# The two expert layers of a top-2 MoE: from split weights in SBUF to weights fetched for each tile

## The chip, the cores and the metric

The kernel runs on one core of one Trainium2 chip. Its time is device microseconds (us) of one execution; the number that counts is the median of several executions, 302.83 us before the change (302.64 to 302.89 in 3 runs). Engines: PE is TensorE (PEld its weight loads), DVE VectorE, ACT ScalarE, POOL GpSimd, SP SyncE; a q behind the name is the engine's sequencer.

## The reference, cut to what matters

Eight batches of 512 tokens with 128 features pass through a small recurrence, which is residual and normalised; then each token goes to its two best experts of eight.

```
x = x + LN(recurrence(LN(x)))                  # two 128x128 layers, relu, a scan
logits = LN(x) @ gate                          # 8 experts, the best 2, softmax of the two
for each token, for each of its 2 experts e:   # w0, w1: 8 x 128 x 512, wo: 8 x 512 x 128, float32
    y = (silu(h @ w0[e]) * (h @ w1[e])) @ wo[e]
x = x + LN(sum of weight * y over the 2)
```

Everything is float32, and the first recurrence and gate decide which experts are taken, so products have to be close to float32.

## The kernel before, in words

Batches are worked off one after another in the **attention part**: layer norm, transpose, two matmuls with a scan between them, residual, second norm, logits, choice of two experts, and for each token its place in a table of rows sorted by expert. POOL sends the rows of each batch there by indirect DMA (`send_row`, L457, 8 per batch). When enough rows of an expert are there, 128 of them make a **tile**: 71 tiles in all (`TILES`). DVE writes for each tile its first row and its expert's first weight chunk (`tile_row_i`, `tile_chunk_i`, semaphore `s_table`, once per phase), and SP loads the rows of a tile into one of 16 ring buffers (`load_tile`, L330 to L333).

The first three batches run before the **loop over slots**: each engine's block first lists that part by hand, in a fixed order, then runs `for k, s, t in slots()`, where slot t works on tile t and its neighbours and, through `a_slot`, on a piece of batches k+3 and k+4 (eight slots per k). Every engine works strictly in its written order, so one waiting instruction holds all behind it.

In a slot PE does: transpose the rows of tile t (`turn_tile`, L1626); both first layers of tile t-1 (`two_layers`); a piece of the attention part; the transposes of `gated` of tile t-2 (`turn_gated`, L1668); the last layer of tile t-3 (`last_layer`, L1684). The product of float32 numbers in the first layers is made from three matmuls of float32r numbers (`layer`, L1631 to L1633): high rows by high weights, low rows by high weights, high rows by low weights. So all weights of w0 and w1 are split before the loop: ACT rounds them (`round_w`, L589), POOL (w0) and DVE (w1, `split_rest`) subtract (L273), and PE with ACT (`low_part`, L1699 and L1701, `take_low`, L595) makes three of the eighths of w1's low part. The rows stand in the array (stationary) and 512 weight columns stream past, so the result has tokens on partitions and must be transposed before the last layer, which contracts over the 512 features. ACT copies x as high part (`first_part`), DVE makes the low part (`rest_part`, L1267); ACT applies silu (`gate_curve`, L633), DVE multiplies (`times_gate_curve`, L1274), ACT copies the transposed result (`gated_turned`, L638) and weighs the output (`take_y`, L648). POOL sends the weighted rows to their pair (`send_y`, L470). After the last tile the pairs are loaded, summed, normalised and added to x.

`fill` (L1693) issues matmuls whose results nobody uses. `late_power` (L435, L438) is the reciprocal root of a variance on POOL; the residual of batch 3, the first in the loop, waits for one.

## Time and profile before

| | us |
|---|---|
| median of 3 runs | 302.83 |
| the profiled execution | 302.5 |
| its span, first to last instruction | 300.8 |
| PE / DVE / ACT / POOL busy in it | 258.3 / 203.0 / 186.8 / 172.5 |
| first transpose of a tile on PE starts at | 58.7 |
| last `take_y` on ACT starts at | 286.4 |

Times inside the profile count from the span's start. Matmuls are pipelined, and their durations overlap: what one costs is the distance from its start to the next start. A float32 matmul appears as two instructions (L1684, x568 for 71 tiles of four matmuls); a float32r matmul and a transpose appear as one. PEclk is the granted clock of TensorE in tenths of full speed (2.4 GHz).

### The profile page before, as it was taken

The page shows a single profiled execution, that of the slowest core. Times are in us where ns is not written, and L with a number is a line of the kernel's source. Part 1 is how long each engine was busy: PE and PEld are TensorE (multiplying, and loading weights), DVE is VectorE, ACT ScalarE, POOL GpSimd, SP SyncE. Part 2 cuts the span into 40 slices and gives each one's busy share as a digit, 9 for nine tenths or more (in the row PEclk, how much of TensorE's full clock was granted, in tenths as well). Part 3 has the DMA queues.
Part 4 walks back from the last instruction along what each step waited for, and adds up shares of the span by engine and source line. Part 5 has one row for each costly group of instructions (what it writes and reads, how often), then busy time and mean ns, then how long its engine had stood idle before and what let it go on. Part 6 is the DMA issues. An engine that isn't in the chain of part 4 may idle for free.

```text
span 300.8 us, 6844 instructions
## 1 busy us (share of the span) xinstructions
PE 258.3 (86%) x1633; PEld 214.1 (71%) x1633; DVE 203.0 (67%) x944; ACT 186.8 (62%) x451; POOL 172.5 (57%) x195
## 2 busy tenths in 40 slices
PE   0646596879999999999999999999999999999800
PEld 0225263448878698898988889888988988888700
DVE  3787998678597559458755955785653433888745
ACT  3666397327665765767684566666566566568681
POOL 7019577757238775874776577777532333357540
PEclk9995559589999999999999999999999999999985
DMA  5999711302111122112212211343333115602137
GB/s 146 153 384 321 210 50 52 89 29 68 50 47 45 46 74 72 44 56 71 74 44 72 74 46 49 97 108 91 100 81 86 43 31 199 263 17 91 49 99 209
DMA packets 28132, 29.57 MB, mean 98 GB/s; under 512 B 4570, under 2 KB 21180, under 8 KB 28096
## 3 DMA queue, kind: packets, MB, share of 16 engines
q1 hardware_dynamic: 22832, 20.04, 23.4%
q0 software_dynamic: 4544, 8.97, 9.3%
q8 instruction: 16, 0.26, 0.4%
q10 hardware_dynamic: 720, 0.13, 0.3%
q14 instruction: 20, 0.16, 0.2%
HBM read 17.53 MB, written 12.05 MB: 98 GB/s over the span
## 4 chain that ended last, share of the span: by engine, by line
PE 71%; DVE 13%; ACT 6%; POOL 4%; issue 4%; DMA 1%; POOLq 0%; DVEq 0%; ACTq 0%
PE bank L1684 19%; PE bank L1631 10%; PE bank L1632 10%; PE bank L1633 10%; PE bank L1668 10%; PE bank L1626 3%; PE bank L1582 2%; PE bank L1554 2%; ACT sb_row L576 1%; PE bank L1575 1%; POOL expert_rows L457 1%; DMA sb_x<-in_L_attn_x 1%; DVE sb_early L864 1%; PE bank L1566 1%; ACT sb_early L548 1%
## 5 line engine op out<-in xcount | busy, mean ns | idle before, releaser
L470 POOL DMA_INDIRECT pair_rows<-sb_y_rows,sb_y_pair x71 | 70.4, 991 | 60.2 <-ACT sb_y_rows L648 41.6
L457 POOL DMA_INDIRECT expert_rows<-sb_row,sb_place x64 | 64.0, 1001 | 23.8 <-issue 16.6
L1684 PE MATMUL bank<-sb_w_raw,sb_gatedT 128*128 x568 | 75.0, 275 | 0.0
L1684 PEld LDWEIGHTS bank<-sb_w_raw,sb_gatedT 128*128 128x128 f32 x568 | 69.1, 192 | 0.2
L1274 DVE TENSOR_TENSOR sb_w_raw<-bank,sb_w_raw 128x512 f32<-128x512 f32 x71 | 48.9, 689 | 29.9 <-PE bank L1633 21.6
L638 ACT ACTIVATE sb_gatedT<-bank 128x512 f32<-128x512 f32 x71 | 42.3, 596 | 37.0 <-PE bank L1668 36.9
L1631 PE MATMUL bank<-sb_w_parts,sb_x_hi 128*128 x142 | 63.0, 444 | 0.3 <-DVE sb_w_raw L1274 0.2
L1632 PE MATMUL bank<-sb_w_parts,sb_x_lo 128*128 x142 | 56.4, 397 | 0.0
L1633 PE MATMUL bank<-sb_w_parts,sb_x_hi 128*128 x142 | 56.1, 395 | 0.0
L633 ACT ACTIVATE sb_w_raw<-bank 128x512 f32<-128x512 f32 x71 | 42.5, 599 | 7.2 <-PE bank L1633 6.0
L1267 DVE TENSOR_TENSOR sb_x_lo<-bank,sb_x_hi 128x128 fp32r<-128x128 f32 x71 | 20.2, 285 | 35.0 <-ACT sb_x_hi L628 34.7
L1668 PE MATMUL bank<-sb_ident,sb_w_raw 128*128 128x128 f32 x284 | 42.9, 273 | 1.1 <-ACT sb_gatedT L638 0.8
L1668 PEld LDWEIGHTS bank<-sb_ident,sb_w_raw 128*128 128x128 f32 x284 | 34.3, 140 | 10.6 <-issue 3.2
L628 ACT ACTIVATE sb_x_hi<-bank 128x128 fp32r<-128x128 f32 x71 | 19.6, 276 | 34.3 <-PE bank L1626 34.2
L1633 PEld LDWEIGHTS bank<-sb_w_parts,sb_x_hi 128*128 128x128 f32 x142 | 26.9, 189 | 6.6
L1631 PEld LDWEIGHTS bank<-sb_w_parts,sb_x_hi 128*128 128x128 f32 x142 | 27.3, 192 | 6.0 <-issue 3.0
L1632 PEld LDWEIGHTS bank<-sb_w_parts,sb_x_lo 128*128 128x128 f32 x142 | 27.2, 192 | 2.9
L648 ACT ACTIVATE sb_y_rows<-bank,sb_y_weight 128x128 f32<-128x128 f32 x71 | 25.7, 363 | 1.5 <-PE bank L1684 1.0
L1626 PE MATMUL bank<-sb_ident,sb_taken_rows 128*128 128x128 f32 x71 | 19.9, 281 | 0.7 <-ACT sb_w_parts L595 0.7
L273 POOL TENSOR_TENSOR sb_w_parts<-sb_w_raw,sb_w_parts 128x512 fp32r<-128x512 f32 x8 | 10.8, 1383 | 14.4 <-ACT sb_w_parts L589 14.4
L576 ACT ACTIVATE sb_row<-sb_x,sb_nm,sb_rs 128x128 f32<-128x128 f32 x32 | 14.3, 488 | 7.0 <-DVE sb_nm L820 7.0
L1566 PE MATMUL bank<-sb_w_outT,sb_early 128*128 128x128 f32 x64 | 11.6, 339 | 6.8 <-DVE sb_early L864 6.8
(194 smaller groups left out, 358.8 us busy)
## 6 DMA issues: line engine op xcount, KB each, us to landing
sb_taken_rows<-expert_rows SPq DMA_DIRECT2D x71, 65.5 KB, 1.9
sb_w_raw<-in_L_ffn_w SPq DMA_DIRECT2D x2, 2048.0 KB, 15.1
sb_w_raw<-pair_rows SPq DMA_DIRECT2D x3, 1024.0 KB, 7.5
out_dram<-sb_x SPq DMA_DIRECT2D x3, 512.0 KB, 3.8
pair_rows<-sb_y_rows,sb_y_pair POOLq DMA_INDIRECT x71, 2.3
sb_x<-in_L_attn_x SPq DMA_DIRECT2D x4, 256.0 KB, 5.9
expert_rows<-sb_row,sb_place POOLq DMA_INDIRECT x64, 2.4
expert_rows<-sb_pad_row SPq DMA_DIRECT2D x8, 65.5 KB
```

The source lines that it names most:

```text
L457: pool.indirect_dma_start(expert_rows[:, :], bass.IndirectOffsetOnAxis(ap=place[b % ROWS][:, k, j:j + 1], axis=0), row[b % ROWS][:, j, :], ...
L470: pool.indirect_dma_start(pair_rows[:, :], bass.IndirectOffsetOnAxis(ap=y_pair[group % 2][:, t % PAIRS:t % PAIRS + 1], axis=0), y_rows[slo ...
L633: act.activation(silu[t % 2][:], p_l1[:], ACT.Silu).then_inc(c["silu"], 1)
L638: act.activation(gatedT[t % 2][:], p_gatedT[:], ACT.Copy).then_inc(c["gatedT"], 1)
L648: act.activation(y_rows[t % Y_SLOTS][:], p_y[t % 2][:, 0:D], ACT.Copy, scale=y_weight[group % 2][:, t % PAIRS:t % PAIRS + 1]).then_inc(c[" ...
L1274: dve.tensor_tensor(gated[t % 2][:], p_l2[:], silu[t % 2][:], ALU.mult).then_inc(c["gated"], 1)
L1626: pe.transpose(p_xeT[:, 0:P], taken_rows[:, t % RING, 0:D], ident[:]).then_inc(c["xeT_ps"], 1)
L1631: pe.matmul(to, x_hi, w_hi, start=True, stop=False)
L1632: pe.matmul(to, x_lo, w_hi, start=False, stop=False)
L1633: return pe.matmul(to, x_hi, w_lo, start=False, stop=True)
L1668: last = pe.transpose(p_gatedT[:, n * P:(n + 1) * P], gated[t % 2][:, n * P:(n + 1) * P], ident[:])
L1684: last = pe.matmul(p_y[t % 2][:, 0:D], gatedT[t % 2][:, n * P:(n + 1) * P], wo.rearrange("p o d -> p (o d)"), start=(n == 0), stop=(n == F ...
```

## The change

Splitting is gone: `w_parts`, `round_w`, `take_low`, `low_part`, `split_rest` and the subtractions on POOL are removed. In `layer` the weights now stand in the array and the rows stream past, with plain float32 matmuls, four per layer of 128 weight columns each; the result comes out with features on partitions, so `turn_gated` and `gated_turned` are removed, and `last_layer` takes `gated` itself, one slot earlier. The weights of a tile are brought together (w0 and w1 of its expert, 128 partitions by 2 times 2 KB) from `w_raw` in SBUF to one of four buffers `w_now` by a DMA that ACT issues two tiles ahead (`chunk_of`, `fetch_w`). `silu`, `gated` and the pairs that are loaded at the end get memory of their own instead of that of `w_raw`. Three `fill`s change, batch 3's second statistics move ahead of the loop, and POOL's power for it too. The diff, without the removed helpers:

```diff
+W_RING = 4
-        silu = [w_raw[:, n * F:(n + 1) * F] for n in (0, 1)]
-        gated = [w_raw[:, n * F:(n + 1) * F] for n in (2, 3)]
+        xeT = pair("xeT", [P, P])
+        silu, gated = pair("silu", [P, F]), pair("gated", [P, F])
+        w_now = [sb(f"w_now{n}", [P, 2, F]) for n in range(W_RING)]
+        pairs_early = sb("pairs_early", [P, 6 * pair_cols])
...
 @block.gpsimd   # before: the four subtractions stood ahead of the sends
-            for n in range(W_SPLITS // 2):
-                pool.wait_ge(s_w_hi, n + 1)
-                first, size = w_split(n)
-                subtract_hi(pool, first, size // 2)
-                subtract_hi(pool, first + size // 2, size // 2).then_inc(s_w0_lo, 1)
             for b in (0, 1):
                 for n in range(K * G):
                     send_row(b, n)
+            late_power(2, 0, ROOT2, mv2[ROOT2 % 2], sd2[ROOT2 % 2], rs2[ROOT2 % 2])
...
 @block.scalar   # eight round_w and three take_low removed from the part before the loop
             def first_part(t):
                 if is_tile(t):
                     act.wait_ge(c["xeT_ps"], t + 1)
-                    act.activation(x_hi[t % 2][:], p_xeT[:, 0:P], ACT.Copy).then_inc(c["x_hi"], 1)
+                    act.activation(xeT[t % 2][:], p_xeT[:, 0:P], ACT.Copy).then_inc(c["xeT"], 1)
+            def chunk_of(t):
+                if not is_tile(t):
+                    return
+                if t == 0:
+                    act.wait_ge(s_w_in[0], 16)
+                    act.wait_ge(s_w_in[1], 16)
+                for p in range(PHASES + 1):
+                    if t == first_tile(p):
+                        act.wait_ge(s_table, p + 1)
+                chunks[t] = act.value_load(tile_chunk_i[0:1, t:t + 1], min_val=0,
+                                           max_val=(E - 1) * FC)
+
+            def fetch_w(t):
+                if not is_tile(t):
+                    return
+                wait(act, c["l2_ps"], t - W_RING + 1)
+                both = w_raw[:, 0:2 * WCOLS].rearrange("p (w c f) -> p w c f", w=2, f=D)
+                act.dma_start(w_now[t % W_RING][:].rearrange("p w (c f) -> p w c f", f=D),
+                              both[:, :, bass.ds(chunks[t], FC), :]
+                              ).then_inc(s_w_now[t % W_RING], 16)
...
             relu(3)
+            chunk_of(0)
+            fetch_w(0)
+            chunk_of(1)
+            fetch_w(1)
             act.activation(unused[:], eps[:], ACT.Silu)
             normalise1(4, 0, G)
-            take_low(2)
 
             for k, s, t in slots():
                 first_part(t)
                 take_y(t - 4)
                 tanh_of_gaps(t)
                 a_slot(k, s, 0)
+                chunk_of(t + 2)
                 gate_curve(t - 1)
+                fetch_w(t + 2)
                 a_slot(k, s, 1)
-                gated_turned(t - 2)
                 a_slot(k, s, 2)
...
 @block.vector
             scan(3)
-            split_rest(LOW_BY_PE, 4)
             top(2)
             choose(2)
-            split_rest(4, 6)
+            start2(3)
             put(2)
             offset1(5)
 
             for k, s, t in slots():
-                rest_part(t)
-                if t == 0:
-                    split_rest(6, 8)
-                elif t == 2:
+                if t == 2:
                     table_start(1)
...
 @block.tensor
-            def layer(to, x_hi, x_lo, first_chunk):
-                w_hi, w_lo = (w_parts[:, bass.ds(first_chunk, FC), part, :] for part in (0, 1))
-                pe.matmul(to, x_hi, w_hi, start=True, stop=False)
-                pe.matmul(to, x_lo, w_hi, start=False, stop=False)
-                return pe.matmul(to, x_hi, w_lo, start=False, stop=True)
+            def layer(to, x, w):
+                for n in range(FC):
+                    last = pe.matmul(to[:, n * P:(n + 1) * P], w[:, n * P:(n + 1) * P], x,
+                                     start=True, stop=True)
+                return last
...
-                n = t % 2
+                n, w = t % 2, w_now[t % W_RING]
+                pe.wait_ge(s_w_now[t % W_RING], 16 * (t // W_RING + 1))
                 wait(pe, c["silu"], t)
-                layer(p_l1[:], x_hi[n][:], x_lo[n][:], chunks[t]).then_inc(c["l1_ps"], 1)
+                layer(p_l1, xeT[n][:], w[:, 0, :]).then_inc(c["l1_ps"], 1)
                 wait(pe, c["gated"], t)
-                if t == 0:
-                    pe.wait_ge(s_w1_lo, 1 + LOW_BY_PE)
-                layer(p_l2[:], x_hi[n][:], x_lo[n][:],
-                      chunks[t] + W_CHUNKS).then_inc(c["l2_ps"], 1)
+                layer(p_l2, xeT[n][:], w[:, 1, :]).then_inc(c["l2_ps"], 1)
...
             times_gate(1)
-            low_part(0)
+            fill(p_l1, 6)
             ranks(1)
             turn1(3)
-            low_part(1)
+            fill(p_l1, 4)
             times_w_in(3)
...
             ranks(2)
-            low_part(2)
-            pe.wait_ge(s_w1_lo, LOW_BY_PE)
             for k, s, t in slots():
                 if is_tile(t - 1):
-                    pe.wait_ge(c["x_lo"], t)
+                    pe.wait_ge(c["xeT"], t)
                 turn_tile(t)
                 if t == 0:
                     pe.wait_ge(a["x1"], 3)
-                    fill(p_y[0], 3)
+                    fill(p_y[0], 2)
                 two_layers(t - 1)
                 a_slot(k, s, 0)
                 chunk_of(t)
-                if t == TILES:
-                    last_layer(t - 3)
-                    turn_gated(t - 2)
-                else:
-                    turn_gated(t - 2)
-                    last_layer(t - 3)
-                if t == 1:
-                    pe.wait_ge(a["x1"], 3)
-                    fill(p_gatedT, 3)
+                last_layer(t - 2)
                 a_slot(k, s, 1)
```

## Rows read from the trace of the kernel before

**Rows 1.** The page: busy us per engine, then the granted clock in 40 slices.
```profile
PE 258.3 (86%) x1633; PEld 214.1 (71%) x1633; DVE 203.0 (67%) x944; ACT 186.8 (62%) x451; POOL 172.5 (57%) x195
PEclk9995559589999999999999999999999999999985
```

**Rows 2.** Stretches: length, PE busy (instructions), granted clock, DMA share, GB/s.
```profile
140.00:160.00 20.00, 20.00 (x136) 1.00 0.18 55
253.00:256.00 3.00, 3.00 (x23) 1.00 1.02 415
```

**Rows 3.** PE in order of time, one tile: start us, us, engine, line, instruction.
```profile
166.77 1.06 PE L1684 MATMUL bank<-sb_w_raw,sb_gatedT 128*128 x8
167.66 0.27 PE L1626 MATMUL bank<-sb_ident,sb_taken_rows 128*128 128x128 f32 x1
...
169.18 0.60 PE L1668 MATMUL bank<-sb_ident,sb_w_raw 128*128 128x128 f32 x4
169.61 0.61 PE L1684 MATMUL bank<-sb_w_raw,sb_gatedT 128*128 x4
```

**Rows 4.** The chain that ended last, one piece: start us, us, what.
```profile
86.20 0.11 PE bank L1626
```

**Rows 5.** DVE in order of time, before the loop and its first slot.
```profile
23.66 0.98 DVE L820 SCALAR_TENSOR_TENSOR sb_nm<-sb_mv,sb_rs 128x4 f32<-128x4 f32 x1
31.33 0.98 DVE L918 TENSOR_TENSOR sb_row<-sb_top 128x4 f32<-128x4 f32 x1
...
42.97 0.15 DVE L918 TENSOR_TENSOR sb_row<-sb_top 128x4 f32<-128x4 f32 x1
...
52.53 0.66 DVE L273 TENSOR_TENSOR sb_w_parts<-sb_w_raw,sb_w_parts 128x512 fp32r<-128x512 f32 x1
...
63.75 1.13 DVE L879 SCALAR_TENSOR_TENSOR sb_x<-bank,sb_rs,sb_x 128x128 f32<-128x128 f32 x4 [1.27 <-POOL sb_rs L438]
```

**Rows 6.** POOL in order of time, before the loop and its first slots.
```profile
27.35 4.94 POOL L273 TENSOR_TENSOR sb_w_parts<-sb_w_raw,sb_w_parts 128x512 fp32r<-128x512 f32 x4 [0.27 <-ACT sb_w_parts L589]
35.48 1.35 POOL L457 DMA_INDIRECT expert_rows<-sb_row,sb_place  x1 [3.19 <-DVE sb_place L971]
...
55.61 1.09 POOL L457 DMA_INDIRECT expert_rows<-sb_row,sb_place  x1 [0.30 <-issue]
...
62.66 1.05 POOL L438 TENSOR_TENSOR sb_rs<-sb_sd,sb_minus_half 128x4 f32<-128x4 f32 x1
```

**Rows 7.** PE in order of time, around the start of the loop.
```profile
58.67 0.47 PE L1626 MATMUL bank<-sb_ident,sb_taken_rows 128*128 128x128 f32 x1 [0.69 <-ACT sb_w_parts L595]
...
60.29 0.77 PE L1631 MATMUL bank<-sb_w_parts,sb_x_hi 128*128 x1
...
70.87 1.02 PE L1554 MATMUL bank<-sb_early,sb_w_inT 128*128 128x512 f32 x2
```

**Rows 8.** ACT in order of time, before the loop.
```profile
50.12 0.59 ACT L595 ACTIVATE sb_w_parts<-bank 128x512 fp32r<-128x512 f32 x1
50.60 0.69 ACT L563 ACTIVATE sb_early<-bank,sb_b_in 128x512 f32<-128x512 f32 x1
```

**Rows 9.** SP's row loads: instruction, count: ns min/median/max, first and last start us.
```profile
L331 SPq TENSOR_LOAD <-sb_tile_row_i x71: 263/268/577, 52.5 to 239.4; - x71
L333 SPq DMA_DIRECT2D sb_taken_rows<-expert_rows x71: 332/333/1237, 53.6 to 240.1; - x71
```

**Rows 10.** The page, DMA issues: KB each, median us from issue to landing.
```profile
sb_taken_rows<-expert_rows SPq DMA_DIRECT2D x71, 65.5 KB, 1.9
sb_early<-pair_rows SPq DMA_DIRECT2D x1, 512.0 KB, 3.4
```

**Rows 11.** All engines in order of time, the last tiles.
```profile
281.54 1.05 PE L1684 MATMUL bank<-sb_w_raw,sb_gatedT 128*128 x8
281.81 0.69 DVE L1274 TENSOR_TENSOR sb_w_raw<-bank,sb_w_raw 128x512 f32<-128x512 f32 x1 [1.14 <-PE bank L1633]
...
286.41 0.37 ACT L648 ACTIVATE sb_y_rows<-bank,sb_y_weight 128x128 f32<-128x128 f32 x1 [0.68 <-PE bank L1684]
```

More of the change, by code:

```diff
@@ L188, in pairs_of @@
                 return early[:, (first - 6) * pair_cols:(end - 6) * pair_cols]
-            return w_raw[:, 4 * F + first * pair_cols:4 * F + end * pair_cols]
+            return pairs_early[:, first * pair_cols:end * pair_cols]
         def half_of_pairs(b, k):
@@ L233, in sandwich_kernel @@
         s_b, s_table = sem("table_step"), sem("table")
-        names_c = ("xeT_ps x_hi x_lo l1_ps l2_ps silu gated gatedT_ps gatedT y_ps y not_first y_pair "
+        names_c = ("xeT_ps xeT l1_ps l2_ps silu gated y_ps y not_first y_pair "
                    "tanh signed y_weight")
         c = {n: sem("c_" + n) for n in names_c.split()}
+        s_w_now = [sem(f"w_now{n}") for n in range(W_RING)]
         s_rows_in = [sem(f"tile_in{n}") for n in range(RING)]
@@ L264, in tiles_of_phase @@
             return range(first_tile(p), first_tile(p + 1) if p < PHASES else TILES)
-        def w_split(n):
-            size = 2 * W_CHUNKS // W_SPLITS
-            return n * size, size
-        def subtract_hi(eng, first, size):
-            span = slice(first, first + size)
-            return eng.tensor_tensor(w_parts[:, span, 1, :], w_raw_chunks[:, span],
-                                     w_parts[:, span, 0, :].bitcast(F32), ALU.subtract)
-        def low_span(n):
-            first, size = w_split(W_SPLITS // 2 + n // 2)
-            return slice(first + n % 2 * size // 2, first + (n % 2 + 1) * size // 2)
-        def low_bank(n):
-            return (bank[1], bank[2], bank[0])[n]
         def x_tile(b, j):
@@ L1162, in last_new @@
                                                         None, ALU.mult))
-            def split_rest(first, end):
-                for n in range(first, end):
-                    start, size = w_split(W_SPLITS // 2 + n // 2)
-                    dve.wait_ge(s_w_hi, W_SPLITS // 2 + n // 2 + 1)
-                    last = subtract_hi(dve, start + n % 2 * size // 2, size // 2)
-                if end == W_SPLITS:
-                    last.then_inc(s_w1_lo, 1)
             def a_slot(k, s, part):
@@ L1647, in two_layers @@
                     return
-                if t == 0:
-                    pe.wait_ge(s_w_hi, W_SPLITS)
-                    pe.wait_ge(s_w0_lo, W_SPLITS // 2)
-                n = t % 2
+                n, w = t % 2, w_now[t % W_RING]
+                pe.wait_ge(s_w_now[t % W_RING], 16 * (t // W_RING + 1))
                 wait(pe, c["silu"], t)
-                layer(p_l1[:], x_hi[n][:], x_lo[n][:], chunks[t]).then_inc(c["l1_ps"], 1)
+                layer(p_l1, xeT[n][:], w[:, 0, :]).then_inc(c["l1_ps"], 1)
                 wait(pe, c["gated"], t)
-                if t == 0:
-                    pe.wait_ge(s_w1_lo, 1 + LOW_BY_PE)
-                layer(p_l2[:], x_hi[n][:], x_lo[n][:],
-                      chunks[t] + W_CHUNKS).then_inc(c["l2_ps"], 1)
-            def turn_gated(t):
-                if not is_tile(t):
-                    return
-                pe.wait_ge(c["gated"], t + 1)
-                wait(pe, c["gatedT"], t)
-                if t == 0:
-                    pe.wait_ge(a["x1"], 3)
-                for n in range(FC):
-                    last = pe.transpose(p_gatedT[:, n * P:(n + 1) * P],
-                                        gated[t % 2][:, n * P:(n + 1) * P], ident[:])
-                last.then_inc(c["gatedT_ps"], 1)
+                layer(p_l2, xeT[n][:], w[:, 1, :]).then_inc(c["l2_ps"], 1)
             def last_layer(t):
@@ L1683, in last_layer @@
                     wo = w_raw_chunks[:, bass.ds(chunks[t] + (2 * W_CHUNKS + n), 1), :]
-                    last = pe.matmul(p_y[t % 2][:, 0:D], gatedT[t % 2][:, n * P:(n + 1) * P],
+                    last = pe.matmul(p_y[t % 2][:, 0:D], gated[t % 2][:, n * P:(n + 1) * P],
                                      wo.rearrange("p o d -> p (o d)"), start=(n == 0),
```

67 lines of the change are left out of this document (6 added, 61 removed).

## The prediction

> **What bounds the kernel now.** I read the page's busy times first: PE is busy 86% of the span, the other engines 57% to 67%, and the granted clock is 9 (full speed, 2.4 GHz) in nearly every slice after the eighth and about half in several before [rows 1]. The stretches then show where PE is the limit: between 140 and 160 us it is busy 20.00 of 20.00 us, while the DMA engines are at 0.18 of their time [rows 2]. So from some 70 us to the last tile only PE's work counts, and ahead of it a chain through all engines. PE in order of time gives one tile: 0.11 us for the transpose of the rows [rows 4], 169.18 - 167.66 - 0.11 = 1.41 for the six passes of the first layers, 169.61 - 169.18 = 0.43 for the four transposes of gated, 167.66 - 166.77 = 0.89 for the last layer [rows 3]; together 2.84 us, the distance of one last layer to the next.
>
> The sum is made against the profiled execution (302.5 us, its span of 300.8 and 1.7 around it). The median of the runs is 0.3 above; that is added at the end.
>
> **The change part by part.**
>
> *Matmuls.* A layer becomes four float32 matmuls with a 128x128 float32 matrix in the array and 128 columns streaming, eight instructions. That is the form of the last layer, also a product over float32 operands of this size: 0.89 us [rows 3]. Two layers cost 1.78 in place of 1.41, and the transposes (0.43) go: 0.11 + 3 x 0.89 = 2.78 per tile, only 0.06 less. The new layers cost 0.37 more than the old; the transposes pay for that. The copy of x's high part stays as a plain copy; the low part on DVE and the copy of the transposed result on ACT lie beside PE, so their removal is worth nothing while PE is full.
>
> *The part before the loop.* Two small DVE instructions of the chain (L820, L918) take 0.98 us each while POOL subtracts, an L918 later only 0.15 [rows 5, 6]; without the subtractions that is 1.66 off the way to the first place table. POOL's first send waited for that table, not for its own subtractions [rows 6], so the sends move by these 1.66, from 35.48 to 33.8, and SP's first row load from 53.6 to 51.9 [rows 9]; its rows land some 0.33 + 1.9 later [rows 9, 10], at 54.2. PE's list reaches the first tile sooner: on ACT the relu of batch 3 stood behind a low-part copy begun 0.48 before it [rows 8], and on DVE one subtraction of 0.66 stood ahead of the choice of batch 2 [rows 5]; with the 1.66 that is 2.8 of the 58.67 [rows 7], and the last low part on PE, with its copy on ACT, goes as well, so the rows are what comes last: first transpose 54.2. The fills that replace the first two low parts are priced at zero change: they stand in the same place and last about as long, and the list behind them waits for DVE anyway.
>
> The weights of tile 0: ACT is past the relu at 50.60 - 1.66 - 0.48 + 0.69 = 49.2; reading the chunk and issuing is, on SP, 53.6 - 52.5 + 0.33 = 1.4 [rows 9]; a load of the same 512 KB lands in 3.4 [rows 10]: 54.0. Hidden by the rows. With a copy of x the first layers of tile 0 start near 55.3 instead of 60.29 [rows 7].
>
> What is late next is batch 3's residual: it stood at 63.75 behind POOL's power [rows 5, 6]. Now the power follows POOL's sixteenth send (55.61 + 1.09 - 1.66 = 55.0), about 1.3 for its two instructions, so the residual runs from 56.5 to 57.6. The first layers of tile 0 take 1.78 at full clock and 3.56 at half; I take 2.9, to 58.2, and PE does not wait for the residual. Then four transposes of batch 4 (0.43), tile 1 (0.11 + 1.78), the last layer of tile 0 (0.89), tile 2 (1.89): 63.3. The same work stands finished before at 70.87 [rows 7]. **Start: 7.5 off.**
>
> *The loop.* From 70.87 to the end of tile 70's first layers, 281.54 [rows 7, 11], are 210.7 us. Of them 68 first layers grow by 0.37 (+25.2), 67 sets of transposes go (-28.8), one last layer moves in (+0.9): **2.7 off**, so this point comes at 63.3 + 208.0 = 271.3.
>
> *The end.* From there to the last take_y are 286.41 - 281.54 = 4.87 now [rows 11], with two sets of transposes, two copies on ACT and three last layers. After the change the last layer of tile 69 runs beside DVE's product (0.27 + 0.69 [rows 11]), then tile 70's (0.89) with some 0.25 for starts: 2.1, **2.8 off**. What follows take_y is the same work, 302.5 - 286.4 = 16.1. Sum: 271.3 + 2.1 + 16.1 = 289.5.
>
> *What the fetches add.* ACT loses a copy of 0.6 per tile and gains a chunk read and an issue. No row shows a DMA issued by ACT between activations. Lower bound zero (its sequencer does it while the engine computes; no gain is possible, since PE is full), upper bound 1.4 per tile in ACT's own time, as on SP [rows 9]. ACT is busy 62% of the span [rows 1] and loses the copy, so on the average even 1.4 fits; in the slot where batch k+3's fourth normalised tile is made just ahead of PE's transposes of it, it would be about 1.0 late, five batches: 5. I take 1.5, nearer to zero, for PE's sequencer reads its own chunk each tile (chunk_of) within a full PE stream [rows 2]. By the Trainium skill, "TensorE: Matmul & The Clock Gate", on the array's architecture, ScalarE's queue holds 8 instructions, so its sequencer may run ahead; no row here shows that, and the sum by it would be zero for this term.
>
> The four buffers are waited for without cost: the buffer of tile t+2 was last read by tile t-2, a slot earlier. The transfers are 524 kB per tile; beside 2.78 us that is 189 GB/s over 55 [rows 2]. The DMA engines moved 415 GB/s when three loads overlapped [rows 2], so a transfer takes 1.3 us of them, 0.45 of their time, and is issued two tiles, nearly 7 us, ahead. In the stretch of those three loads near the end both compete for some 10 us; bound 0 to 2, I take 0.3. ACT's read of tile 5's chunk waits for the second table in slot 3: 0 to 1, I take 0.2. Sum: 289.5 + 1.5 + 0.3 + 0.2 = 291.5, and 0.3 for the median: **291.8**.
>
> **The rivals.**
>
> *The start does not come forward.* PE is 7 us early, but the place tables, POOL's sends ((55.61 - 35.48) / 15 = 1.34 each [rows 6]) and batch 3 move by 1.7 only; PE would then stall in the first eight slots for them, above all if the clock stays at half. For it: four engines must keep step over ten microseconds. Against: followed step by step none came later than PE. Only the 1.7 is left: 291.8 + 5.8 = 297.6.
>
> *ACT pays in full* for reading and issuing, the 5 of above in place of 1.5: 295.3. Against it speaks ACT's idle share [rows 1].
>
> *The transfers do not overlap* (slower than before). If each fetch takes the 3.4 us of a lone 512 KB load [rows 10] and the next begins only then, tile 70's weights are there at 50.6 + 71 x 3.4 = 292, and 1.8 + 2.1 + 16.1 follow: 312. It costs time from some 3 us per fetch on, and from 3.27 on the kernel is slower than before. For it: no transfer from SBUF to SBUF stands in the trace. Against: 415 GB/s with overlap. The Trainium skill, "DMA: Bandwidth & Descriptors", on the anatomy of one DMA, gives 2.0 us plus the bytes at 436 GB/s; an estimate by it for 524 kB is 3.2 us, which one at a time would give about 298. The three overlapping loads disagree with taking it as a pace.
>
> *The layers do not run at the last layer's rate.* 16 x 71 instructions depend on its 0.111 us; at 0.121 the whole gain is gone, at 0.13 it is 313. Against: same shapes, same types.
>
> **How the numbers follow.** Forecast 0.50, start 0.17, ACT in full 0.17, transfers 0.12, rate 0.04. The forecast's own range is 287.5 to 294.5; with the first two rivals 286.5 to 302, which leaves out the two slower cases and a little below. About 0.2% (0.6 us) is what a measurement can tell from no change. Faster 0.83, same 0.03, slower 0.14.
>
> **What would show it.** First transpose of a tile near 54 and the first layers near 55; batch 3's residual near 57; slots without attention work 2.78 apart on PE, with 16 instructions 0.11 apart; last take_y near 275; the fetches issued on ACT in 0.3 to 0.45 us and landing in 2 to 4; DMA share near 0.6. PE waiting for a DMA would prove the transfers rival, ACT ending PE's waits in slots 3 to 6 the second, DVE or POOL ending them before 85 us the first. Wrong is the forecast if PE has more than 2 us of waits after its first layers.

## The result, and the profile after

The changed kernel takes 308.81 us (median of 6 runs, 307.44 to 310.55) beside 302.63 for the kernel before on the same chip: ratio 1.0207, 95% interval 1.0173 to 1.0241. It is slower by 2%, where 291.8 was forecast. The profiled execution took 310.55, its span 308.8.

The page of the kernel after, busy time per engine, and in 40 slices PE's busy tenths and the granted clock:

```profile
PE 257.2 (83%) x2056; PEld 239.3 (77%) x2056; DVE 182.8 (59%) x868; ACT 140.3 (45%) x368; POOL 163.2 (53%) x187
...
PE   0668664799999999999999999994999999499900
...
PEclk9995598599999999999999999999899999789975
```

PE is busy 1.1 us less than before [rows 1], but its row has two holes, in the 28th and the 35th slice, and the clock drops behind them. The row of the kernel before has neither:

```profile
PE   0646596879999999999999999999999999999800
```

The rest of PE's work in the loop is as forecast. One tile on PE in order of time, quiet slot:

```profile
166.03 0.27 PE L1572 MATMUL bank<-sb_ident,sb_taken_rows 128*128 128x128 f32 x1
166.14 1.95 PE L1577 MATMUL bank<-sb_xeT,sb_w_now 128*128 128x128 f32 x16
167.93 1.06 PE L1613 MATMUL bank<-sb_w_raw,sb_gated 128*128 x8
168.82 0.27 PE L1572 MATMUL bank<-sb_ident,sb_taken_rows 128*128 128x128 f32 x1
```

From one transpose to the next 2.79 (forecast 2.78; before 2.84 [rows 3]): 0.11, then 1.79 for both first layers, 0.89 for the last. PE in order of time at the start of the loop:

```profile
55.19 0.47 PE L1572 MATMUL bank<-sb_ident,sb_taken_rows 128*128 128x128 f32 x1 [2.68 <-DMA sb_taken_rows<-expert_rows]
...
57.22 3.62 PE L1577 MATMUL bank<-sb_xeT,sb_w_now 128*128 128x128 f32 x16
...
66.08 1.06 PE L1613 MATMUL bank<-sb_w_raw,sb_gated 128*128 x8
```

The work that before was done at 70.87 [rows 7] is done at 66.08: 4.8 earlier, not 7.5. PE waits for rows until 55.19, which were forecast for 54.2, and the first layers of tile 0 take 3.42 of PE's time. What DVE and POOL were to do came as forecast: POOL's first send (forecast 33.8), and batch 3's residual (forecast 56.5 to 57.6).

```profile
33.80 1.33 POOL L435 DMA_INDIRECT expert_rows<-sb_row,sb_place  x1 [26.70 <-DVE sb_place L938]
```

```profile
56.03 1.13 DVE L846 SCALAR_TENSOR_TENSOR sb_x<-bank,sb_rs,sb_x 128x128 f32<-128x128 f32 x4 [1.60 <-POOL sb_rs L416]
```

What PE waited for in all, kernel after: us in total, times, longest.

```profile
PE bank L1572 <- DMA sb_taken_rows<-expert_rows: 8.4, 6, 4.0
...
PE bank L1577 <- DMA sb_w_now<-sb_w_raw: 4.7, 1, 4.7
```

13.1 us of waits for transfers, of which some 10 come after tile 0's first layers; the forecast called 2 us of waits there the point from which it is wrong. The two holes, first the one at tile 48, the first tile of the last phase, PE in order of time:

```profile
215.05 0.45 PE L1572 MATMUL bank<-sb_ident,sb_taken_rows 128*128 128x128 f32 x1 [4.01 <-DMA sb_taken_rows<-expert_rows]
215.29 3.39 PE L1577 MATMUL bank<-sb_xeT,sb_w_now 128*128 128x128 f32 x16
```

Before that phase SP writes eight blocks of 128 padding rows (the pads), one behind another, waits until they have landed, and only then loads rows. SP's DMA instructions in order of time (the second number of a line is from the first to the last), after:

```profile
196.92 11.13 SPq L320 DMA_DIRECT2D expert_rows<-sb_pad_row  x8
213.09 5.89 SPq L311 DMA_DIRECT2D sb_taken_rows<-expert_rows  x6
```

and the same in the kernel before:

```profile
198.11 8.52 SPq L342 DMA_DIRECT2D expert_rows<-sb_pad_row  x8
209.95 9.31 SPq L333 DMA_DIRECT2D sb_taken_rows<-expert_rows  x9
```

The chain of waits after has the last pad's landing in it, and the row load behind it (start us, us, what):

```profile
207.71 4.17 DMA expert_rows<-sb_pad_row
...
213.09 1.82 DMA sb_taken_rows<-expert_rows
```

SP reads each pad's address into a register first; those reads take 0.271 to 1.072 us, median 0.444, where before they took 0.263 to 0.378, median 0.270. So eight pads cost 11.13 in place of 8.52 (2.6 more), and from the last of them to the row load it is 5.0 in place of 3.3 (1.7 more). The first pad leaves 1.2 earlier, so the row load leaves 3.1 later, while PE is free 3.5 earlier (211.04 for 214.55). PE waits 4.01, and its next first layers run with the clock granted at 0.61 in the mean of the four us around it:

```profile
140.00:160.00 20.00, 20.00 (x176) 19.43 (x174) 11.09 (x50) 10.18 (x27) 15.68 (x17) 1.00 0.62 213
214.00:218.00 4.00, 2.95 (x14) 2.98 (x15) 0.00 (x0) 1.14 (x3) 0.98 (x1) 0.61 0.27 67
253.00:256.00 3.00, 3.00 (x30) 3.00 (x29) 0.66 (x2) 1.13 (x3) 1.47 (x2) 1.00 0.77 229
260.00:270.00 10.00, 5.29 (x34) 5.05 (x33) 4.33 (x19) 1.84 (x4) 1.95 (x2) 0.80 0.94 360
```

(Stretches of the kernel after: length, busy time of PE, PEld, DVE, ACT and POOL, granted clock, DMA share, GB/s.) In the quiet stretch the DMA engines are at 0.62 and 213 GB/s where they were at 0.18 and 55 [rows 2]. The second hole is ahead of tile 65: PE waits for the weights of tile 63 (tiles count from 0; the expectations below call it the fetch of tile 64). The chain shows the transfer, PE's rows what it cost:

```profile
255.37 11.36 DMA sb_w_now<-sb_w_raw
```

```profile
266.77 3.78 PE L1577 MATMUL bank<-sb_xeT,sb_w_now 128*128 128x128 f32 x16 [4.71 <-DMA sb_w_now<-sb_w_raw]
270.35 1.92 PE L1613 MATMUL bank<-sb_w_raw,sb_gated 128*128 x8
```

It was issued 2.15 us behind the first of the three pair loads (SP, 253.22). From 253 to 266.7 the DMA engines moved some 4.6 MB (229 GB/s to 256, 316 to 261, 402 to 266, then 408); what was issued between 252.3 and 260.9 is 3.15 MB of pairs and four fetches, 2.1 MB. The packets, counted by queue (q1 is SP's, q10 ACT's; packets, MB, share of 16 engines), show how this fetch went. From 255.4 to 260.5 ACT's queue has no line in the view, so it moved nothing, and SP's moved nearly half of the pairs:

```profile
q1 hardware_dynamic: 375, 1.47, 90.4%
```

From 260.5 to 265.2 both moved, nearly packet for packet, 2 KB against 4 KB:

```profile
q1 hardware_dynamic: 299, 1.16, 63.1%
q10 hardware_dynamic: 267, 0.53, 29.1%
```

So the first packet came 5.2 us after the issue; over all 71 fetches the median is 1.3. What held ACT's queue no run shows. The fetch landed at 266.7, the three pair loads 6.7, 11.5 and 14.6 after their issues, the last at 269.2. DMA issues of the page after (KB each, median us to landing; before 1.9 for the rows [rows 10], and 7.5 for the pairs, on its page):

```profile
sb_taken_rows<-expert_rows SPq DMA_DIRECT2D x71, 65.5 KB, 2.7
...
sb_pairs_early<-pair_rows SPq DMA_DIRECT2D x3, 1024.0 KB, 11.5
```

The end of the loop, PE's last 16 and ACT's last `take_y`:

```profile
291.80 2.27 PE L1613 MATMUL bank<-sb_w_raw,sb_gated 128*128 x16
...
294.11 0.37 ACT L623 ACTIVATE sb_y_rows<-bank,sb_y_weight 128x128 f32<-128x128 f32 x1 [0.84 <-PE bank L1613]
```

So the forecast's pieces measure, in the profiled execution: start point 66.1 (63.3), loop 225.7 (208.0), end 2.3 (2.1), what follows 16.4 (16.1). The miss is the loop, and a little the start.

### The profile page after: what moved, and what is told of

It reads as the page before. It is cut to its first block, busy times and chain, and to the rows that moved or that the text cites. A ratio compares the mean times of both kernels' runs of the same rounds, so it can differ in the third digit from the quotient of the medians.

```text
span 308.8 us, 7588 instructions
## 1 busy us (share of the span) xinstructions
PE 257.2 (83%) x2056; PEld 239.3 (77%) x2056; DVE 182.8 (59%) x868; ACT 140.3 (45%) x368; POOL 163.2 (53%) x187
## 4 chain that ended last, share of the span: by engine, by line
PE 43%; DMA 13%; POOL 12%; issue 11%; DVE 8%; SPq 7%; ACT 3%; ACTq 2%; POOLq 0%; DVEq 0%
PE bank L1577 24%; PE bank L1613 11%; POOL expert_rows L435 9%; DMA sb_w_now<-sb_w_raw 4%; SPq L309 3%; DMA expert_rows<-sb_row,sb_place 2%; DMA sb_taken_rows<-expert_rows 2%; POOL pair_rows L448 2%; SPq L318 2%; PE bank L1572 2%; DMA sb_b_in<-in_L_attn_b_in 2%; PE bank L1512 1%; PE bank L1528 1%; DMA expert_rows<-sb_pad_row 1%; PE bank L1500 1%
## 5 line engine op out<-in xcount | busy, mean ns | idle before, releaser
L1577 PE MATMUL bank<-sb_xeT,sb_w_now 128*128 128x128 f32 x1136 | 144.2, 282 | 5.0 <-DMA sb_w_now<-sb_w_raw 4.7
L1577 PEld LDWEIGHTS bank<-sb_xeT,sb_w_now 128*128 128x128 f32 x1136 | 137.9, 198 | 6.6 <-DMA sb_w_now<-sb_w_raw 4.9
L1224 DVE TENSOR_TENSOR sb_gated<-bank,sb_silu 128x512 f32<-128x512 f32 x71 | 49.0, 690 | 85.1 <-PE bank L1577 61.3
L1613 PE MATMUL bank<-sb_w_raw,sb_gated 128*128 x568 | 77.2, 279 | 0.6 <-issue 0.3
L1613 PEld LDWEIGHTS bank<-sb_w_raw,sb_gated 128*128 128x128 f32 x568 | 69.9, 194 | 2.0 <-issue 1.7
L586 ACT ACTIVATE sb_xeT<-bank 128x128 f32<-128x128 f32 x71 | 19.6, 276 | 87.7 <-PE bank L1572 86.6
L591 ACT ACTIVATE sb_silu<-bank 128x512 f32<-128x512 f32 x71 | 42.4, 598 | 35.9 <-PE bank L1577 33.8
L1572 PEld LDWEIGHTS bank<-sb_ident,sb_taken_rows 128*128 128x128 f32 x71 | 10.7, 151 | 11.0 <-issue 6.8
L1512 PEld LDWEIGHTS bank<-sb_w_outT,sb_early 128*128 128x128 f32 x64 | 10.4, 240 | 7.7 <-DVE sb_early L831 7.6
L1500 PE MATMUL bank<-sb_early,sb_w_inT 128*128 128x512 f32 x16 | 11.4, 802 | 2.7 <-DVE sb_early L823 2.7
## 6 DMA issues: line engine op xcount, KB each, us to landing
sb_pairs_early<-pair_rows SPq DMA_DIRECT2D x3, 1024.0 KB, 11.5
```

The lines of the kernel that those rows point to most:

```text
L586: act.activation(xeT[t % 2][:], p_xeT[:, 0:P], ACT.Copy).then_inc(c["xeT"], 1)
L591: act.activation(silu[t % 2][:], p_l1[:], ACT.Silu).then_inc(c["silu"], 1)
L1224: dve.tensor_tensor(gated[t % 2][:], p_l2[:], silu[t % 2][:], ALU.mult).then_inc(c["gated"], 1)
L1500: pe.matmul(p_first(b)[:], w_inT[:], mixed[b % 2], start=True, stop=True).then_inc(a["hidden_ps"], 1)
L1512: last = pe.matmul(p_first(b)[:, j * D:(j + 1) * D], states[b % 2][:, j * P:(j + 1) * P], w_outT[:], start=False, stop=(j == G - 1))
L1572: pe.transpose(p_xeT[:, 0:P], taken_rows[:, t % RING, 0:D], ident[:]).then_inc(c["xeT_ps"], 1)
```

## The experiments

Theory A, formed from this trace: PE, DVE, POOL and ACT do what was forecast, and the loss is late transfers, above all at two places (pads before tile 48, pair loads before tile 65), because 37.3 MB more go through the same DMA engines. Rivals: the cost is ACT's, for reading and issuing in every slot; or the new first layers cost more than they seem to; or the bytes cost the same time wherever they are moved. All ratios are to the kernel before (302.6 to 302.8 beside them), with 95% intervals. The *step* of a tile is the time from the transpose of the tile before it on PE to its own.

**Without the transfers.** Tiles take expert 0's weights from where they stand in SBUF; the choice of the expert in the first layers is left out.

```diff
-                pe.wait_ge(s_w_now[t % W_RING], 16 * (t // W_RING + 1))
-                layer(p_l1, xeT[n][:], w[:, 0, :]).then_inc(c["l1_ps"], 1)
+                layer(p_l1, xeT[n][:], w_raw[:, 0:F]).then_inc(c["l1_ps"], 1)
...
-                chunk_of(t + 2)
-                fetch_w(t + 2)
```

> The changed kernel without any weight transfer: both first layers use expert 0's weights in place, with fixed addresses, so the choice of the expert in them is left out; the same matmuls in the same order. Theory A (what the prediction missed is what 71 transfers of 512 KB do to the other transfers, and PE's tile of 2.79 us, the earlier start and the shorter end are real): no wait for weights, pads issued in 8.5 us as before the change, wait ahead of tile 48 under 2, time 293 to 296. Rival C (the new form of the layers, the order of slots or PE's clock costs the time): 304 or more.

Measured: 290.90 (289.98 to 291.50), ratio 0.9601 (0.9577 to 0.9625). PE, then ACT, in order of time, and PE's waits for transfers:

```profile
53.66 0.48 PE L1566 MATMUL bank<-sb_ident,sb_taken_rows 128*128 128x128 f32 x1 [0.94 <-DMA sb_taken_rows<-expert_rows]
...
64.03 1.06 PE L1609 MATMUL bank<-sb_w_raw,sb_gated 128*128 x8
...
272.31 2.27 PE L1609 MATMUL bank<-sb_w_raw,sb_gated 128*128 x16
```

```profile
274.62 0.37 ACT L623 ACTIVATE sb_y_rows<-bank,sb_y_weight 128x128 f32<-128x128 f32 x1 [0.84 <-PE bank L1609]
```

```profile
PE bank L1566 <- DMA sb_taken_rows<-expert_rows: 0.9, 1, 0.9
```

Start point 64.0, loop 208.3, end 2.3, what follows 16.3: within 0.7 of each forecast term. The time is below the 293 to 296 that theory A expected, and far from rival C's. Matmuls, start and end were priced right; the 17.9 us between this kernel and the changed one are what the transfers add.

**A quarter of the bytes.** As many transfers, reads and issues, but 128 KB each; three quarters of the weights of the first layers are left out. DVE clears the four buffers at the start of the kernel.

```diff
-                act.dma_start(w_now[t % W_RING][:].rearrange("p w (c f) -> p w c f", f=D),
-                              both[:, :, bass.ds(chunks[t], FC), :]
+                act.dma_start(w_now[t % W_RING][:].rearrange("p w (c f) -> p w c f", f=D)[:, :, 0:1, :],
+                              both[:, :, bass.ds(chunks[t], 1), :]
...
 @block.vector
+            for w in w_now:
+                dve.memset(w[:], 0.0)
```

> The changed kernel with each transfer cut to its first 128 of 512 columns of both layers (128 KB, rows of 512 bytes); the other columns stay zero, so three quarters of the weights are left out. As many issues on ScalarE, a quarter of the bytes. Theory A by bytes: between the kernel without transfers and the changed one, nearer the first, the wait of tile 64 under 1, time 294 to 298. Rival D (the count of transfers, their issue on ScalarE and their place in the queues matter, not the bytes): 304 or more.

Measured: 295.59 (294.37 to 296.51), ratio 0.977 (0.9738 to 0.9802). 4.7 of the 17.9 us are left, 26%: the loss goes with the bytes, not with the issues. The quiet slots stay at 2.79 in it and in the changed kernel, so ACT's read (median 0.55) and issue (0.63) of one transfer per slot cost nothing there. At the start this kernel can't be compared: the first transpose is as late (55.56) as in the changed one, but the four memsets, 0.91 us each, come first on DVE, and POOL's first send leaves at 34.83 in place of 33.80. That is some 1.1 of the 4.7 against the kernel without transfers (33.69). Beside the pair loads a quarter of the bytes is not a quarter of the time: the same fetch took 8.14, and PE waited 0.9 for it.

```profile
245.65 8.14 DMA sb_w_now<-sb_w_raw
```

**The pair loads in turn.** SP waits for each of the three before it issues the next.

```diff
                 load_pairs(g)
+                sp.wait_ge(s_pairs_in[g], 16)
```

> The changed kernel with one edit: SP waits for each of the three 1 MB loads of the pairs to land before it issues the next. Theory A (a weight fetch issued behind three outstanding 1 MB loads gets through only when they do, 11.36 us instead of some 3): PE's wait of 4.7 us for the fetch of tile 64 and the half clock after it go, tile 65 comes 6 to 7.5 us earlier, time 301.5 to 303. Rival B (the fetch is late because ScalarE issues it late or because a fetch is slow at any time): the wait stays within 1 us of 4.7 and the time near 308.8.

Measured: 308.13 (306.96 to 308.46), ratio 1.0161 (1.0138 to 1.0184). A miss: tile 65's step is 3.14, but the stall has moved. PE of this kernel, in order of time:

```profile
269.65 3.93 PE L1578 MATMUL bank<-sb_xeT,sb_w_now 128*128 128x128 f32 x16 [1.76 <-DMA sb_w_now<-sb_w_raw]
...
279.88 1.16 PE L1578 MATMUL bank<-sb_xeT,sb_w_now 128*128 128x128 f32 x8 [1.61 <-DVE sb_gated L1225]
```

First a fetch is late beside these loads (step of tile 67: 6.69), then DVE waits in its order for the pairs (8.0 us in three waits), and PE for DVE (tile 69: 5.03). Order alone didn't help while the same bytes are due in the same 20 us.

**Four pads by ACT.** SP writes four of the eight, ACT the others, one per slot.

```diff
-                    for e in range(E):
+                    for e in range(E // 2):
...
+                pad(t - FULL_TILES + STEP)
```

> The changed kernel with one edit: four of the eight pad writes ahead of the last phase are issued by ScalarE, one in each of the slots 40 to 43, the other four by SP as before. Theory A (the rows of tile 48 are late because SP issues the pads one after another for 11.13 us and they land 4.17 us after the last): the first row load of the last phase starts at 207 to 209 instead of 213.1, PE's wait of 4.0 us ahead of tile 48 falls under 1 and the half clock after it goes, time 303 to 305. Rival B (the last phase waits for the rows of batch 7 or its table): the row load still starts after 211, time near 308.8.

Measured: 304.07 (303.05 to 305.62), ratio 1.0049 (1.0028 to 1.0071). A hit: SP's first row load of the last phase leaves at 206.78 in place of 213.09, tile 48's step is 2.79 (6.96), the next 2.79 (4.37); tiles 44 to 46, beside the pads, lose 0.7 over 2.79 each, together. The stall at tile 65 stays, its transfer again in the chain of waits:

```profile
248.40 10.83 DMA sb_w_now<-sb_w_raw
```

**Fetches further ahead.** Eight buffers in place of four, and ACT's lead grows from two tiles to six after tile 50, so that the last transfers are issued before the pair loads.

```diff
-W_RING = 4
+W_RING = 8
...
+            def ahead(t):
+                return 2 if t < 50 else min(6, 3 + (t - 50) // 2)
...
-                chunk_of(t + 2)
+                now = range(ahead(t - 1) + t, ahead(t) + t + 1)
+                for u in now:
+                    chunk_of(u)
                 gate_curve(t - 1)
-                fetch_w(t + 2)
+                for u in now:
+                    fetch_w(u)
```

> Eight weight buffers in place of four, and from tile 50 on the transfers run ahead by three, then up to six tiles in place of two, so that those of the last tiles are issued before the three 1 MB pair loads; the same bytes in all. Theory A (a fetch issued beside the pair loads is late, the bytes themselves have room earlier, where the DMA engines are half idle): the step of 10.3 us at tile 65 falls below 3.5, the stall at tile 48 stays (6.9 and 4.4), 301.0 to 302.5. Rival B (the bytes cost the same wherever they are moved, as when the pair loads were issued in turn): the wait moves to the rows of tiles 50 to 65 or to the last pairs, 306 to 309.

Measured: 305.51 (304.24 to 306.02), ratio 1.0088 (1.0058 to 1.0118). Between the two: tile 65's step is 2.87, but the steps of tiles 52 to 59 are 3.5 us over 2.79 each, together.

**Both.** The lead and the four pads by ACT in one kernel.

> The transfers run ahead as above, and four of the eight pad writes are issued by ACT instead of SP. Theory A (the two stalls are two separate late transfers, and are the greater part of the loss): both go, no step beyond 3.6 after tile 8, last first layers some 10 us earlier than in the changed kernel, 296.0 to 298.0; what is left against 290.9 without any fetch is the start (2) and the phase starts (2.7). Rival B (they share the bandwidth, so that what is saved at tile 48 is lost at tile 65): 301 to 304.

Measured: 301.10 (299.19 to 301.22), ratio 0.9948 (0.9931 to 0.9964). Better than before by 0.5%, but 3 short of what was expected, and again in the fifties: 3.5 us over 2.79 a step. What ACT waited for between 220 and 235 us of it, and its DMA issues around one silu:

```profile
ACT sb_silu L591 <- issue: 4.5, 4, 1.5
```

```profile
218.45 1.47 ACTq L615 DMA_DIRECT2D sb_w_now<-sb_w_raw  x2
```

Four silus wait for ACT's own sequencer. Where the lead grows, a slot holds two reads and two issues, 2 x (0.55 + 0.63) at the medians with register work between them, ahead of or beside its activations, and that no longer fits into 2.79. In the changed kernel, from 140 to 160 us, the same wait is 0.3 once.

**The second fetch later.** As the last one, and tile 1's weights are fetched in slot 0, not ahead of the loop.

```diff
             chunk_of(0)
             fetch_w(0)
-            chunk_of(1)
-            fetch_w(1)
...
+            chunk_of(1)
...
+                if t == 0:
+                    fetch_w(1)
```

> As the kernel with both stalls taken away, and the transfer of tile 1's weights is issued in slot 0 instead of ahead of the loop, so that one 512 KB transfer instead of two lies beside the first row load. Theory A (the first rows land late because of these transfers): the first transpose goes from 55.2 towards the 53.7 without fetches, by 0.8 to 1.5, and the time is 0.5 to 1.5 below its companion's. Rival B (the first row load waits for POOL's sends, which the transfers delay elsewhere, or for its own issue): the first transpose stays within 0.3 and the time is the same, or up to 1 longer, since tile 1's weights come later.

Measured: 298.79 (298.31 to 299.71), ratio 0.9881 (0.9863 to 0.9899): 1.2% faster than the kernel before, and no other here that does all the work is better by more than its interval. It is 2.3 below its companion, more than theory A's 0.5 to 1.5. First transpose and its wait on PE:

```profile
54.03 0.48 PE L1591 MATMUL bank<-sb_ident,sb_taken_rows 128*128 128x128 f32 x1 [1.75 <-DMA sb_taken_rows<-expert_rows]
```

In the kernels with two whole transfers ahead of the loop it was at 55.1 to 55.5, in those with one at 54.0 to 54.7, without any at 53.66. POOL's first send moves by up to 0.8 among these; counted from it, that is 21.4 to 21.6, 20.6 to 21.0 and 20.0. Between 251 and 261 us, where pair loads and the rest meet, PE is not held:

```profile
251.00:256.00 5.00, 5.00 (x46) 4.99 (x46) 2.85 (x7) 2.66 (x8) 1.36 (x2) 1.00 1.01 361
256.00:261.00 5.00, 5.00 (x47) 5.00 (x46) 4.37 (x21) 1.90 (x6) 1.95 (x2) 1.00 1.03 402
```

Four fetches, those of tiles 67 to 70, still leave behind the first pair load (250.94 to 258.63 for 248.03), and the first of them begins 4.4 us after its issue; with a lead of six tiles PE does not wait for them. With the same bytes as in the changed kernel, 10.0 of the 17.9 us are gone: the rival by which the bytes cost the same wherever they are moved falls.

**The last six transfers by SP**, between its last row load and the pair loads; ACT issues one per slot again.

```diff
+            for t in range(TILES - 6, TILES):
+                chunk = sp.value_load(tile_chunk_i[0:1, t:t + 1], min_val=0, max_val=(E - 1) * FC)
+                wait(sp, c["l2_ps"], t - W_RING + 1)
+                sp.dma_start(...)   # as fetch_w
```

> As the kernel with the late second fetch (pad writes on two queues, eight buffers), but ACT issues one transfer per slot, two tiles ahead, as in the changed kernel, and the last six are issued by SP between its last row load and the three 1 MB pair loads. Theory A (the 2.5 to 3 us that the slots of tiles 52 to 59 lost when ACT ran ahead are ACT's: two reads and two issues in one slot are longer than 2.79): every step from tile 50 to tile 64 is 2.79 to 2.9, and the time is 1.5 to 3 below 298.8: 296.0 to 297.3. Rival B (those slots lost time to the bytes, which shared the DMA engines with rows and pads): the loss moves to tiles 60 to 70, where six more transfers now lie in 13 us, and the time is 298.5 to 300.5.

Measured: 307.52 (306.47 to 310.56), ratio 1.0178 (1.0142 to 1.0214). The first half holds: from tile 50 to 64 all steps are 2.79 but two (3.05 and 2.96). That fits a loss by ACT, though fewer bytes moved there too (from 231 to 236 us 267 GB/s, where the kernel of 298.79 had 344). The sum is a miss, by a wait that neither theory had: SP works in its order too, its transfers wait 7.6 us in all for buffers, and the pair loads leave behind the sixth, at 256.25 instead of 248.03. SP, and what DVE waited for:

```profile
241.34 14.74 SPq L340 DMA_DIRECT2D sb_w_now<-sb_w_raw  x6
256.25 2.71 SPq L353 DMA_DIRECT2D sb_pairs_early<-pair_rows  x3
```

```profile
DVE sb_pairs_early L1278 <- DMA sb_pairs_early<-pair_rows: 10.2, 1, 10.2
```

DVE waits 10.2 for the pairs in front of the next `gated`; tile 65's step is 13.38.

**Twelve buffers**, so that SP issues those six among its last row loads.

```diff
-W_RING = 8
+W_RING = 12
...
+                    if t == TILES - 3:
+                        for u in range(TILES - 6, TILES - 2):
+                            fetch_late(u)
                     load_tile(t)
+            fetch_late(TILES - 2)
+            fetch_late(TILES - 1)
```

> As the kernel whose last six transfers were issued by SP, but with twelve buffers in place of eight, so that SP issues them one per slot between 227 and 241 us, among its last row loads, and the pair loads are not behind them. Theory A (the 13.4 us step at tile 65 was DVE, which waits in its order for the pairs, whose loads SP issued 8 us later than before and while its own transfers were moving; ACT's doubled issues were the loss of tiles 52 to 59): pair loads issued near 248, no step above 3.1 from tile 50 on but that of tile 54 and 69, 295.5 to 297.3. Rival B (rows, pads, pairs and two transfers per slot are more than the DMA engines move, near 380 of the 415 GB/s seen): steps of 3.3 or more among tiles 55 to 66 that end in a wait for a DMA, 298 to 303.

Measured: 304.25 (303.67 to 305.56), ratio 1.0052 (1.0032 to 1.0071), above both ranges. The trace is from one more execution:

> The same kernel as the one whose last six transfers SP issues among its last row loads (304.7 us, no usable trace of it yet), for a trace. Theory A (the last pair loads or rows are late because SP, which works in order, holds them behind transfers that wait for buffers): one step of 4 to 8 us that ends in a wait for rows or, through DVE, for pairs. Rival B (the DMA engines are full between 227 and 256 us): several steps of 3.3 to 5 us, DMA share at 0.95 or more through the stretch.

306.48 in this one run. SP did not spread the six over its row loads: four leave from 236.25 on, ahead of the last three row loads, two behind them, and the pair loads leave at 251.68, not near 248. Tile 62's step is 4.91 and tile 65's 9.07; PE waits 2.9 for weights, 3.4 for DVE, which waits 6.0 for pairs. Stretches of 5 us, columns as above:

```profile
241.00:246.00 5.00, 5.00 (x48) 5.00 (x47) 1.55 (x5) 1.87 (x6) 1.96 (x2) 1.00 1.03 369
246.00:251.00 5.00, 3.15 (x28) 2.91 (x27) 1.01 (x4) 1.74 (x5) 1.84 (x2) 1.00 1.04 355
251.00:256.00 5.00, 5.00 (x47) 5.00 (x46) 1.16 (x2) 1.73 (x4) 1.07 (x2) 1.00 1.03 356
256.00:261.00 5.00, 3.98 (x36) 3.75 (x35) 0.22 (x1) 1.51 (x5) 1.00 (x2) 1.00 1.01 355
261.00:266.00 5.00, 1.95 (x11) 1.76 (x10) 3.69 (x16) 0.85 (x2) 0.00 (x0) 0.66 1.03 416
```

The DMA engines are full for 25 us, and what is issued into that lands late, first weights, as rival B had it, though not in several steps; then pairs that left 3.7 later than in the kernel of 298.79, which is theory A's wait through DVE. From 241 to 246 PE is not held beside 369 GB/s; this, too, speaks for ACT as the cause of the loss at tiles 52 to 59.

**A lead of four** on ACT in place of six, otherwise the kernel of 298.79.

```diff
-                return 2 if t < 50 else min(6, 3 + (t - 50) // 2)
+                return 2 + (t >= 52) + (t >= 58)
```

> As the kernel with the late second fetch, but ACT's lead grows from two tiles to four instead of six, so that two slots instead of four hold two reads and two issues. Theory A (a slot with two costs ACT some 0.5 to 1.0 us, and what is gained near the pair loads needs only two more tiles of lead): 296.5 to 298.5, first to second. Rival B (fetches of tiles 69 and 70, issued after the pair loads, are late again by the 11 us that such a fetch took): a step of 4 to 9 us at tile 68 to 70, 300 to 305.

Measured: 298.66 (297.67 to 301.11), ratio 0.989 (0.9847 to 0.9934), the same as with six. Tiles 50 to 59 lose 0.6 in place of 3.7, but tiles 60 to 66 lose 2.3 in place of nothing: 1.0 at tiles 60 to 62, behind ACT's second slot with two transfers, whose silus wait 0.7 to 1.5 for ACT's sequencer, and 1.3 at tiles 65 and 66, where DVE waits 1.9 for pairs. Rival B did not show: PE never waits for weights near the end, and no step of tiles 68 to 70 is above 3.

## Why the prediction was wrong, point by point

*The matmuls* were right: 2.79 per tile, 16 instructions at 0.11, the transposes gone. The rival by which the layers do not run at the last layer's rate fell.

*The start* was half right. The tables, POOL's sends and the residual came as worked out, and the rival by which they would stall PE did not show. Without transfers the point is 64.0 (forecast 63.3; the rest is tile 0's layers and the four transposes behind them at half clock, 3.4 in place of 2.9 and 0.7 in place of 0.4). The 54.2 for the rows counted the issue's 0.33 twice, since the 1.9 runs from the start of the issue; without transfers they come at 53.7. With transfers the point is 66.1: "Hidden by the rows" was right for the weights, but the rows themselves, priced at 1.9 from a trace without such transfers, took 2.7, and their load left 0.7 later than without transfers (52.43 for 51.76), mostly for SP's read ahead of it, 1.1 for 0.5.

*The loop without transfers and the end* were right, 208.3 for 208.0 and 2.3 for 2.1.

*The step that failed is the term "What the fetches add"*: 2.0 us forecast (1.5 for ACT, 0.3 beside the pair loads, 0.2 for the table), 17.9 measured between the medians with and without. By tile, from the two profiled executions (310.55 and 290.94): 2.0 at the start, 2.7 from tile 4 to 47, mostly where a phase begins and PE waits for rows; 5.75 at tiles 48 and 49; 7.5 at tile 65; the rest, 1.6, in single steps after tile 49. These make 19.6, since the profiled execution of the changed kernel was its longest. Inside it:

- *"In the stretch of those three loads near the end both compete ... bound 0 to 2, I take 0.3"*. It cost 7.5. The sentence ahead of it sets the pace of the transfers (1.3 us each by 415 GB/s) against a lead of nearly 7 us. What counted here is what was in flight beside it: 3.15 MB and its own half at the 316 to 402 GB/s of the stretch are 9 to 12 us, and it took 11.36; with a quarter of its own bytes still 8.14. Then PE runs 16 instructions at half clock, 3.58 in place of 1.79, and the last layer of the tile before is slow as well: 4.71 + 1.79 + 0.8 = 7.3 of the 7.5, for a wait of 4.71. The rate for this stood in the trace of before, 415 GB/s while the three loads of 1 MB were moving [rows 2]; by it alone the sum is 8.8, two more than the lead.
- *The pads are not in the prediction at all.* It asked what is late next at the start of the loop, and not of SP's chains further on. The rows behind the pads landed 1.9 after 209.95 in the kernel before, and PE took them at 214.55: 2.7 of slack. PE came 3.5 earlier, the row load 3.1 later. When ACT shares the pads, nothing of these 5.75 us is left at tiles 48 and 49, 0.7 come in at tiles 44 to 46, and the time falls by 4.7.
- *ACT* (1.5) was too much for one transfer per slot: no quiet slot is longer than 2.79, and of the slots with attention work from tile 4 to 47 only those of tiles 16, 24 and 40 (0.5 to 0.7, the phase starts) and 37 (0.3) are more than 0.2 longer than without transfers. By the Trainium skill, "TensorE: Matmul & The Clock Gate", on the array's architecture, ScalarE's queue holds 8 instructions; the prediction inferred that its sequencer may run ahead, and the sum by that was zero. The trace agrees as long as there is one transfer per slot, and shows its end where there are two (4.5 us of waits in a stretch of 15).

*"The transfers do not overlap"* gave the right sign (312) for a reason that did not hold: one every 2.79 us went through, at 213 GB/s in the quiet stretch, without any wait of PE. (What the prediction cites from the Trainium skill, "DMA: Bandwidth & Descriptors", on the anatomy of one DMA, is a fit for DMAs that POOL issues; these are ACT's.) The mechanism was a third one: lateness at the few places where other large or chained transfers are due. By the Trainium skill, "DMA: Bandwidth & Descriptors", on queues, rings and completion order, each DMA engine takes turns among its queues, and the increment of a semaphore lands only after every earlier write of that engine, across its queues. By the first half the fetch, alone on ACT's queue and with packets of 2 KB against 4 KB, would have needed about three times its own bytes, an estimate of 1.57 MB at the 395 GB/s of 260.5 to 265.2, some 4 us. From 260.5 on it went like that, in 4.7; the 5.1 us before, in which ACT's queue moved nothing, are not explained by it. In all eight kernels in which ACT issues every fetch, the first fetch beside the pair loads began 4.2 to 5.2 after its issue. The second half did not make the fetch wait for all the pairs: it landed at 266.7, the last of them at 269.2. So what holds ACT's queue stays open; that the loss goes with the bytes in flight is shown.

Also open: how the 2.0 us at the start divide between the bytes and ACT's issues ahead of the loop (counted from POOL's first send, the first transpose comes at 20.7 with a quarter of the bytes, about halfway between 20.0 without transfers and 21.4 with whole ones), and the 2.7 up to tile 47, which no run took apart.

## What to carry to other kernels

A transfer is priced by its place, not by its pace: add up the bytes that are in flight when it is issued, divide by what the engines have been seen to move, and compare that with its lead. Here a queue of its own did not keep the fetch out of the way: beside loads of 1 MB on SP's queue it began 4.2 to 5.2 us after its issue, in place of 1.3. Do this for every other transfer that now shares the engines too, above all for chains in one engine's order (read, issue, wait for landing), whose slack must be looked up, because a faster engine uses it up from the other side. And a wait of PE costs more than its length when the clock falls in it: 5.75 us for one of 4.0, 7.5 for one of 4.7.

## What the runs showed of the hardware that was not expected

- Reading one register from SBUF took 0.27 us on SP in the median before the change, with the DMA engines at 0.18 of their time from 140 to 160 us; with the transfers the pads' reads took 0.44 in the median and up to 1.07, and ACT's up to 0.98 (1.45 where the lead grew).
- Issuing the weights' transfer took 0.63 us on ACT, the rows' 0.33 on SP.
- PE's waits of 4.0 and 4.7 us, and one of 1.8 when the pairs were loaded in turn, were each followed by one tile's first layers at half clock or near it (rows of 3.4 to 3.9 us in place of 1.95; granted clock 0.50 to 0.61 around them); those of 0.3 to 0.5 at the phase starts were not, nor the one of 0.9 with a quarter of the bytes (a row of 2.05, granted clock 1.00).
- Run to run the changed kernel spreads by 1% (307.44 to 310.55), the kernel before by 0.1% (302.46 to 302.89).
